# Row maxima of attention round 0 inside the projection stage, those of round 1 inside round 0

## The reference

```
x = x + s * g                                    # end of layer 0
xn = _layernorm(x)
Q = (xn @ Wq.T + bq) * scale; K = (xn @ Wk.T + bk) * scale; V = xn @ Wv.T + bv    # 16 heads of 16
scores = where(causal, Q @ K^T, -inf)            # per sequence of 1024 and head
attn = softmax(scores); out = attn @ V; s = out @ Wo.T + bo
```

## Time and profile before

| | us |
|---|---|
| median of 3 runs (lowest, highest) | 1851.57 (1850.24, 1861.25) |
| the profiled execution | 1867.35 |
| its span, first to last instruction | 1865.6 |
| busy: PE, DVE, ACT, POOL | 1618.1, 1373.3, 1032.9, 672.2 |
| mean granted clock of TensorE | 0.936 of full |

### The profile page before, as it was taken

How to read it: one execution, slowest core, us unless ns; L and a number is a source line. 1 busy time by engine, 2 the same in 40 slices (tenths; PEclk the granted TensorE clock), 3 DMA queues, 4 the chain that set the end, 5 groups by cost and what they waited for, 6 DMA issues and landing times. The chain is left out here.

```text
span 1865.6 us, 34560 instructions
## 1 busy us (share of the span) xinstructions
PE 1618.1 (87%) x9650; PEld 1253.5 (67%) x9650; DVE 1373.3 (74%) x3710; ACT 1032.9 (55%) x2457; POOL 672.2 (36%) x842
## 2 busy tenths in 40 slices
PE   6897787679983776999999999997889999988997
PEld 5786676569982554554555555544789999967775
DVE  6778999256667887999888888832666666657777
ACT  2555465246664761466576767664556666643443
POOL 2545588410007633121236767620000000056662
PEclk9898899889995996899999999998999999999998
DMA  9322456654444887242354546414964444355552
GB/s 345 120 69 68 96 134 183 173 162 131 132 123 138 275 298 210 58 110 62 70 125 134 175 135 176 129 40 133 274 186 133 131 132 132 119 158 170 164 167 77
DMA packets 291879, 272.72 MB, mean 146 GB/s; under 512 B 138153, under 2 KB 260714, under 8 KB 289644
## 3 DMA queue, kind: packets, MB, share of 16 engines
q1 hardware_dynamic: 267960, 215.41, 39.9%
q0 software_dynamic: 18432, 50.36, 8.9%
q10 hardware_dynamic: 5332, 4.96, 0.8%
HBM read 136.84 MB, written 133.69 MB: 145 GB/s over the span
## 5 line engine op out<-in xcount | busy, mean ns | idle before, releaser
L1880 ACT ACTIVATE ca_PT<-ca_psS 128x512 f32<-128x512 f32 (+3 forms) x768 | 336.4, 494 | 206.0 <-PE ca_psS L1917 201.0
L1421 POOL DMA_INDIRECT g_y<-ys_scratch,pos x128 | 125.0, 977 | 434.7 <-POOLq L73 363.7
L1796 DVE CUSTOM_DVE_ANT_0 ca_masked_row<-ca_psM,mask_row 128x384 f32<-128x384 f32 (+3 forms) x512 | 224.2, 485 | 44.8 <-PE ca_psM L1900 42.7
L1917 PE MATMUL ca_psS<-ca_QS,ca_KS 128*128 128x512 f32 (+1 forms) x480 | 175.4, 369 | 1.4 <-ACT ca_PT L1880 1.4
L1800 DVE TENSOR_REDUCE ca_part<-ca_psM 128x1 f32<-128x512 f32 x256 | 163.6, 684 | 17.0 <-PE ca_psM L1900 15.6
L1929 PE MATMUL ca_psO<-ca_PT,ca_VA 128*17 128x512 f32 (+3 forms) x1536 | 163.1, 497 | 6.0 <-ACT ca_OT L1872 6.0
L790 PE MATMUL fa_psO<-fa_weighed,ident 128*128 128x256 f32 x512 | 132.0, 416 | 38.1 <-DVE fa_weighed L585 38.1
L1900 PE MATMUL ca_psM<-ca_KS,ca_QS 126*128 126x512 f32 (+2 forms) x480 | 159.5, 380 | 5.5 <-DVE ca_part L1796 4.3
L1917 PEld LDWEIGHTS ca_psS<-ca_QS,ca_KS 128*128 128x128 f32 x480 | 90.8, 190 | 87.4 <-ACT ca_PT L1880 58.5
L790 PEld LDWEIGHTS fa_psO<-fa_weighed,ident 128*128 128x128 f32 x512 | 104.9, 210 | 59.8 <-DVE fa_weighed L585 44.4
L391 POOL DMA_INDIRECT xs_scratch<-x_sb,pos x128 | 124.6, 973 | 55.9 <-ACT ca_PT L1880 34.2
(11 more groups left out here) (271 smaller groups left out, 4656.1 us busy)
## 6 DMA issues: line engine op xcount, KB each, us to landing
xs_scratch<-fa_blank SPq DMA_DIRECT2D x32, 640.0 KB, 4.9
x_sb<-xs_scratch SPq DMA_DIRECT2D x143, 128.0 KB, 2.1
ys_scratch<-x_sb SPq DMA_DIRECT2D x143, 128.0 KB, 1.7
xs_scratch<-fa_blank SPq DMA_DIRECT2D x32, 384.0 KB, 6.7
spare<-qk_scratch SPq DMA_DIRECT2D x24, 512.0 KB, 7.4
ca_QS<-qk_scratch SPq DMA_DIRECT2D x20, 512.0 KB, 6.2
ca_KS<-qk_scratch SPq DMA_DIRECT2D x20, 512.0 KB, 7.8
x_sb<-in_ffn SPq DMA_DIRECT2D x16, 608.0 KB, 4.1
```

The costliest lines, as they stand in the source:

```text
L1421: pool.indirect_dma_start(y[:, t % R, k, :], None, y_dram, bass.IndirectOffsetOnAxis(pos[:, t, k:k + 1], 0)).then_inc(got[t % R], 16)
L1796: ins = dve.tensor_tensor_reduce(masked_row[:, (n * NU + u) % BANKS, h * w:(h + 1) * w], bank[:, h * w:(h + 1) * w], mask_row[:, CHUNK - w ...
L1880: act.activation(PT[:, s % PTS, h, off:CHUNK], psS[(GH * s + h) % BANKS][:, off:CHUNK], ACT.Exp)\
L1917: pe.matmul(psS[tile % BANKS][:, off:CHUNK], KS[slot][:, h, kt * P:(kt + 1) * P], QS[slot][:, h, c * CHUNK + off:(c + 1) * CHUNK], start=T ...
```

## The change

Units of round 0 now run in the projection stage. MAXIMA_UNITS is made global; `units_of(n)` deals the 38 units over steps 27 to 44, about one for each of two places in a step. PE runs the first half before `features` and the second half behind; DVE takes the second half of the step before behind `low_half`, and the first half of this step before `qk_low_half`. All units go through a single bank, psM, and psK shrinks from four banks to three. SP loads the stacks of round 0 in `fetch`, at step FETCH = 8 + 5 + 1 + 8 + 1 = 23. The values of round 0 are pulled in attention. The mask is made by POOL at the head of the stage, and mask_row and part are held across both stages; to make room, rot_a and rot_b of the first attention have one buffer in place of two, and POOL there waits for its own last addition.

In attention DVE starts with whole(0) and negate(0). All 38 units of round 1 run in steps 2 to 6 of round 0 (`ahead_first`), before which PE waits for slots 0 and 1. KS[1] is zeroed by ACT instead of POOL, and SP sends the maxima of round 0 ahead of the loads of slot 1.

```diff
-        psT, psV, psK = ps("psT", [P, HID], 2), ps("psV", [P, CHUNK], 2), ps("psK", [P, CHUNK], BUFS)
+        psT, psV, psK = ps("psT", [P, HID], 2), ps("psV", [P, CHUNK], 2), ps("psK", [P, CHUNK], KBANKS)
+        psM, = ps("psM", [P, CHUNK], 1)
...
+    FETCH, UNITS_AT, LAST = BASE + QK_LAG + 1 + SPAN * QK_TILES + 1, 27, TILES + BASE + QK_LAG
+    def units_of(n):
+        wide = 2 * (LAST - UNITS_AT)
+        halves = [range(NU * k // wide, NU * (k + 1) // wide) for k in (2 * (n - UNITS_AT), 2 * (n - UNITS_AT) + 1)]
+        return halves if UNITS_AT <= n < LAST else [(), ()]
...
# gpsimd, head of the stage
+            pool.memset(mask_row[:, :], 0.0).then_inc(mask_blank, 1)
+            pool.wait_ge(mask_blank, 1)
+            pool.affine_select(out=diagonal, ...).then_inc(mask_done, 1)
...
# vector
+            def unit(u):
+                qt, k0, w, h0, nh = MAXIMA_UNITS[u]
+                dve.wait_ge(unit_done, u + 1)
+                ... (the reductions of the unit in attention, from psM into part) .then_inc(unit_out, 1)
-            steps((5, inverse_root), (BASE, normalise), (BASE + 1, low_half), (1, combine), (BASE + 2, values), (3, residual),
-                  (BASE + QK_LAG + 1, qk_low_half))
+            steps((5, inverse_root), (BASE, normalise), (BASE + 1, low_half), (None, units_before), (1, combine), (BASE + 2, values),
+                  (3, residual), (None, units_behind), (BASE + QK_LAG + 1, qk_low_half))
...
# tensor
-                if k >= BUFS:
-                    pe.wait_ge(qklo_out, k - (BUFS - 1))
+                if k >= KBANKS:
+                    pe.wait_ge(qklo_out, k - (KBANKS - 1))
+            def unit(u):
+                if u == 0:
+                    pe.wait_ge(first_in, 16 * (LOADS - 1))
+                else:
+                    pe.wait_ge(unit_out, u)
+                for h in range(nh):
+                    ins = pe.matmul(psM[:, h * w:(h + 1) * w], first_slot[0][0:STACK, h0 + h, qt * P:(qt + 1) * P],
+                                    first_slot[1][0:STACK, h0 + h, k0:k0 + w], start=True, stop=True, skip_group_check=True)
+                ins.then_inc(unit_done, 1)
-            steps((BASE, transpose), (BASE + 1, values_and_logits), (BASE + QK_LAG, features))
+            steps((BASE, transpose), (BASE + 1, values_and_logits), (None, units_before), (BASE + QK_LAG, features), (None, units_behind))
...
# sync
-            sp.wait_ge(zeroed, 2)
-            for m in range(QK_TILES):
-                sp.wait_ge(qk_stored[m], 32 * SPAN)
-                sp.wait_ge(v_stored[m], 16 * POS_TILES // BUFS)
-            load_stacks(sp, qk_dram, 0, first_slot[0], first_slot[1], first_in)
+            def fetch(n):
+                if n == FETCH:
+                    sp.wait_ge(zeroed, 2)
+                    for m in range(QK_TILES):
+                        sp.wait_ge(qk_stored[m], 32 * SPAN)
+                    load_stacks(sp, qk_dram, 0, first_slot[0], first_slot[1], first_in)
+            steps((3, keep), (BASE + 2, save), (BASE + 2, store_v), (BASE + QK_LAG + 1, store_qk), (None, fetch))
...
# attention, sync
+            sp.wait_ge(filled, 1)
+            one_key_rows(0)
             maxima_rows(0, 0)
+            pull_values(0)
+            sp.wait_ge(zeros_done, 1)
+            sp.wait_ge(keys_zeroed, 1)
+            pull(1)
+            one_key_rows(1)
+            sp.wait_ge(zeros_done, 3)
+            one_key_rows(2)
...
# attention, vector
+            whole(0)
+            negate(0)
             for at in range(FRONT):
                 route(at)
-            dve.wait_ge(masked, 1)
-            for u in range(NU):
-                unit(0, u)
-            whole(0)
-            negate(0)
-            for u in range(FIRST):
-                unit(1, u)
...
# attention, tensor
-            pe.wait_ge(stack_in[0], 16 * LOADS)
-            for u in range(NU):
-                unit(0, u)
             transpose_maxima(0)
-            pe.wait_ge(stack_in[1], 16 * LOADS)
-            for u in range(FIRST):
-                unit(1, u)
-            pe.wait_ge(ones_done, 16 * SLOTS)
                 for s in range(NS):
+                    if n == 0 and s == FIRST_STEP:
+                        pe.wait_ge(stack_in[0], 16 * LOADS)
+                        pe.wait_ge(stack_in[1], 16 * LOADS)
```

More of the change, by code:

```diff
@@ L1165, in steps @@
         def steps(*stages):
-            for n in range(TILES + max(lag for lag, _ in stages)):
+            for n in range(TILES + max(lag for lag, _ in stages if lag is not None)):
                 for lag, stage in stages:
-                    if lag <= n < TILES + lag:
+                    if lag is None:
+                        stage(n)
+                    elif lag <= n < TILES + lag:
                         stage(n - lag)
@@ L1607, in load_stacks, with causal_attention @@
         sp.dma_start(KS[half:P:APART, :, :].rearrange("p h n -> p (h n)").bitcast(F32), rows[1]).then_inc(loaded, 16)
-def causal_attention(nc, qk_dram, v_dram, ident, mask_row, m_dram, ao_dram, logits, before, every, tile_ids, pos, wts, te,
+def causal_attention(nc, qk_dram, v_dram, ident, mask_row, part, m_dram, ao_dram, logits, before, every, tile_ids, pos, wts, te,
                      sig, rows, xs_dram, sent, early, o_tile, wo_dram, bo_dram, w_dram, first_slot, first_in):
@@ L1632, in causal_attention @@
         PT = sb("PT", [P, PTS, GH, CHUNK])
-        units = [(qt, k0, w, h0, min(CHUNK // w, GH)) for qt in range(POS_TILES)
-                 for k0, w in [(k, min(CHUNK, (qt + 1) * P - k)) for k in range(0, (qt + 1) * P, CHUNK)]
-                 for h0 in range(0, GH, min(CHUNK // w, GH))]
+        units = MAXIMA_UNITS
         NU = len(units)
@@ L1647, in causal_attention, with units_ahead @@
         assert NS * GH % SLOTS == 0 and NS % PTS == 0
+        ahead_first = [list(range(NU * max(s - FIRST_STEP, 0) // (WHOLE - FIRST_STEP), NU * max(s + 1 - FIRST_STEP, 0) // (WHOLE - FIRST_STEP)))
+                       for s in range(WHOLE)] + ahead[WHOLE:]
+        def units_ahead(n, s):
+            later = n + 1 + s // WHOLE
+            return [(later, u) for u in (ahead if n else ahead_first)[s]] if later < ROUNDS else []
         COPY, TURN, USE = (WHOLE - 1, 2), (WHOLE + 2, 3), (WHOLE + 3, 4)
         last_step = [max(s for s, (c, _, _) in enumerate(steps) if c == cc) for cc in range(SPAN)]
-        part = sb("part", [P, SPAN, GH, POS_TILES])
         maxima = sb("maxima", [P, GH, POS_TILES])
@@ L1691, in _ @@
             pool.memset(one_rows[:, :], 1.0).then_inc(filled, 1)
+            pool.memset(QS[1][:, :, :].bitcast(F32), 0.0).then_inc(zeros_done, 1)
             routing.ranks(pool)
-            for stack in (QS, KS):
-                pool.memset(stack[1][:, :, :].bitcast(F32), 0.0).then_inc(zeros_done, 1)
-        masked = masks(nc, mask_row, (ctx, block))
         @block.sync
@@ L1803, in whole @@
             def whole(n):
[L1804 removed]
+                if n:
+                    dve.wait_ge(unit_out, n * NU)
                 lower, upper = part[:, 0, :, :], part[:, 1, :, TPC:]
@@ L1834, in step @@
             def step(n, s):
-                todo = [(n + 1 + s // WHOLE, u) for u in ahead[s] if n + 1 + s // WHOLE < ROUNDS]
+                todo = units_ahead(n, s)
                 for k in todo[:1]:
@@ L2029, in build @@
             first_slot = list(spans(spare[:, :], (GH, SEQ), (GH, SEQ)))
+            mask_row, part = sb(held, "mask_row", [P, CHUNK]), sb(held, "part", [P, SPAN, GH, POS_TILES])
             before, every = sb(held, "before", [P, P]), sb(held, "every", [P, P])
```

103 lines of the change are left out of this document (60 added, 43 removed).

## The result

The changed kernel takes **1885.03 us** (median of 4 runs, 1876.36 to 1889.88) against 1852.62 us (4 runs, 1850.24 to 1861.25) on the same chip: a ratio of **1.014 [1.011, 1.017]**, some 26 us slower. The profiled execution took 1889.88 us, its span is 1887.8: 22.2 more than before's 1865.6, at a granted clock of 0.940 (before 0.936).

A forecast was written before the change was run, and what follows sets the result against it. DVE was taken as the limit from attention's first unit, no single engine at the projection stage's end. Terms 0.3 + 3 + 18.3 - 1.1 - 16.5 = +4.0 us on 1851.57 gave 1855.6 us, range 1841 to 1870, chance 0.55.

The forecast's parts named there:

- After the barrier: Start of attention to a point in round 0: scores 7 us after the barrier, units at 18, gain 16.5 us.
- my bounds: Limits on the gain after the barrier: -12 if loads land later or DVE is less full, -20 if better.
- Loads at step 23: Projection stage: four early 512 KB loads make one gathered row pair 3 us late, +3 us, between 0 and +10.
- stores held up: Rival: stores of steps 24 to 26 wait behind the loads and delay buffer reuse; +10, 1862 us, chance 0.11.
- Units in the stage: Steps 27 to 44: 38 units through one bank add 5.6, 6.2 and 6.5 us, together +18.3.
- the turn through the bank: Late stage steps: DVE waits while PE refills the single bank; a unit left over pays a whole turn, 1.2 us.
- DVE's floor: Steps 41 to 44 with DVE working without a gap: 3.3 + 9 x 0.60 = 8.7 us.
- floor of +10: Steps 27 to 44 if DVE works without a gap: the stage grows by only 10 us.
- Barrier, small edits: Barrier no longer waits for load issues, -1.1 us; mask +0.3; three psK banks and single rotation buffers 0.
- PE's clock: Rival: PE's clock falls to the half level in steps 35 to 44; +17, 1873 us, chance 0.07.
- The range: Whole kernel: from -11 to +18 us, 1841 to 1870 us.

The follow-up runs named there:

- e6: Changed kernel with DVE's copy written as a two-operand maximum and the m_hi cast taken straight from PSUM, POOL's memsets left in place: 1.0068 of the kernel before, 1871.34 us.
- e1: Changed kernel with POOL's three large memsets delayed until the first maxima are split: 1.0077 of the kernel before, 1873.86 us.
- e12: Kernel before with only the loads of round 0's stacks moved, to step 31: 0.9999 of the kernel before.
- e2: Kernel before with only the four loads of round 0's stacks moved, to step 23: 1.0034 of the kernel before.
- e3: Changed kernel with two psM banks used in turn and psK cut from three to two: 1.0084 of the kernel before, 1875.45 us.
- e11: Kernel before with round 0's loads at step 31 and only its last ten units in steps 35 to 44, one a step: 0.9998, 1857.77 us.
- e4: Changed kernel without the units of round 0, their maxima left at zero, all else kept: 1.0033 of the kernel before.
- e8: Kernel before with one extra DVE copy at the start of attention, while POOL runs memsets: 1860.64 us in one profiled run.

## Why the prediction was wrong

**After the barrier: the step that failed.** "Whole and negate for round 0 come first, some 2.4 us", and 1.2 us of DVE for them; hence scores at 7, units at 18, -16.5. In place of the 2.4 us, the maxima left 11.5 us after the barrier (743.74 to 755.26), because the copy and the cast came under POOL's memsets. Scores came at 16.5 us, units at 29.2: 11.2 of the 13.2 us missed. Of these the hold is 9.2 to 9.5: without it, in e6, units come at 19.7, still 1.7 later than forecast. The last 2.0 are the rate: 30.16 us of DVE's work in 34.61, 0.87, where I took the 0.95 of before's round 0; TensorE's granted clock is 0.82 there, in the earlier trace rows 0.92, and e6 has the same 35.0 us at 0.79. e1 and e6 bring the scores to 7.3 us and 7.4 us and `negate(1)` 11.8 and about 12.5 us ahead of before, at the weak end of my bounds (-12 to -20); the 4 us short of -16.5 are these two terms and not the hold. Their ratios fall from 1.0142 to 1.0077 and 1.0068, 12 to 14 us, some more than the hold's 9 in the profiles, with intervals of about 8 us. That this hold is the cause of the largest part is shown, by taking away the cover, by changing the form, and by making it in the kernel before.

No rival of mine contained it. The price of `whole` and `negate` came from a place where no memset ran, 749.3 us, and I had named POOL's memsets only as something that loads wait for. What moves to another place must be priced beside its new neighbours. The Trainium skill (SBUF — State Buffer, Who interferes with whom) has the rule: copy and cast can use a pair of SBUF ports that VectorE shares with GpSimd, which one of them holds for a whole instruction, and tensor_tensor and tensor_reduce do not meet a GpSimd memset there. The runs agree: 3.53, 6.24 and 7.54 us held; 0.16 (e6's tensor_tensor) and 0.69 (the router's tensor_reduce under a memset of the kernel before) not. That the ports are the reason is the Trainium skill's; the runs show the forms.

**Loads at step 23.** Mechanism right (a gather late, ACT waits, DVE behind it), size wrong: 5.3 us alone, 6.4 in the changed kernel, for 3; inside the bounds of 0 and 10. I had one gather 3 us late; ACT waited 7.6 for it. The rival "stores held up" isn't it here: one store landed 11.6 us after its issue, as the rival's condition wants, but no wait of ACT for a stored buffer stands among those from 650 to 742. With the loads at step 31, in e12, it is what happens: ACT waits 7.8 us for stored buffers. By the Trainium skill's rule on rings (DMA: Bandwidth & Descriptors, Queues, rings and completion order) I had the gathers keep their turn; the runs don't agree for step 23, gathers landed after up to 10.1 us (8.9 in e2), though late stores there were too.

**Units in the stage.** +19.5 for +18.3; by parts +6.3, +6.4, +5.2 and 1.5 at step 45, for 5.6, 6.2 and 6.5. Right in size. In steps 41 to 44 also in mechanism: e3 removes the turn through the bank and reaches DVE's floor. In steps 35 to 40 the 3.3 us came out (3.37 to 3.45, one step of 4.69, the last of 2.87), but the mechanism was not the bank alone: e3 with two banks and e11 with one unit a step have the same length; the loop through PE's values, read from e11's timeline, fits both and wasn't tested by itself. The Trainium skill's rule on rotating banks (Perfetto Trace Analysis, Matmuls), by which I had the whole stage fall to its floor of +10, is worth 4.3 us here, most of it in steps 41 to 45, where nothing else orders the two engines.

**Barrier, small edits.** -1.4 for -1.1: right. psK with three banks: about 1 us at most by e4. POOL's wait in the rotation lies in the first attention; no run takes it out. The +3.3 ahead of step 23 can't be told from scatter: in e2, e8 and e12, whose code up to there is before's, the mark lies at 637.3, 638.3 and 634.3 us, in before at 644.4.

**PE's clock.** The rival is refuted: 1.00 in steps 35 to 44, in spite of PE's waits. But the clock does fall earlier: it is 0.50 in step 27, behind the step of 10.0 us in which PE waits, and 0.90 over steps 27 to 34, where before had 1.00. e2 and e4 have the same 0.50 in step 27 and steps 27 to 45 of 53.8 and 54.8 us, so without units it costs little; with units its price isn't separated.

**The range.** Its lower half rested on a gain behind the barrier of at least 12 us. With -3.3 in that term alone the forecast would have been +17, 1869; with the loads' 3.4 and the stage's 1.2 as well, +22, and that is the span's difference. Two sums of the working are off by little: the floor of the range, 0.3 + 10 - 1.1 - 19, is -9.8 and not -11, and from 723.58 to 736 it is 12.4 us and not 12.2. Neither changes the outcome.

## What to carry to other kernels

Price moved work by its neighbours in the new place: a short copy or cast on DVE that starts under POOL's memsets costs what the memsets have left, and another form of the same work (two operands, or from PSUM) costs nothing of it. Work put into an engine's idle time is hidden only if nothing else in the step waits for it in turn; here 23 us of units in a stage with 12.6 us of idling cost 18 to 19.5. And transfers moved to a stretch where DMA engines are 0.88 busy are not free because their issue is: 2 MB cost 5.3 us there at once, by late gathers. Moved eight steps later they cost as much stage time in the profile, by late stores at its end; so look for the price as far as the engines stay full, and not only in the steps behind the issue.

## What the runs showed of the hardware

A one-operand copy or cast of DVE from SBUF to SBUF, in fp32, doesn't end while POOL's memset of 128x4096 runs, and isn't let in between two memsets in a row: 6.24 and 7.54 us, where it takes 0.21 and 0.17 alone. In the probe the copy's record even starts 0.10 us before the first memset's. Meanwhile PE, ACT and the other forms on DVE run at their usual times, and the memsets themselves take 3.50 us with or without a waiting copy. The held instruction counts as busy: a DVE at 14.91 of 16.54 us was in truth stopped for 9.4, and only the mean duration of its group shows it.
